# Layernorm gain and shift moved from ScalarE's copies to VectorE, and a fill from ScalarE to GpSimd

## The reference

```python
def _layernorm(x, w, b):
    mu = jnp.mean(x, axis=-1, keepdims=True)
    var = jnp.mean((x - mu) ** 2, axis=-1, keepdims=True)
    return (x - mu) * jax.lax.rsqrt(var + EPS) * w + b
ln1_out = _layernorm(hidden_states, ln1_weight, ln1_bias)
qkv = jnp.einsum('sbh,oh->sbo', ln1_out, qkv_weight)
...
hidden_after_attn = hidden_states + proj_out
ln2_out = _layernorm(hidden_after_attn, ln2_weight, ln2_bias)
x = ln2_out.reshape(-1, H)
logits = jnp.einsum('th,eh->te', x, router_weight)
...
return hidden_after_attn + moe_out
```

## Time and profile before

| | |
|---|---|
| median of 3 runs | 3438.64 us (3434.58 to 3450.35) |
| profiled execution, its own time | 3450.35 us, span 3448.6 |
| mean granted TensorE clock | 0.931 |
| busy over the span | PE 3024.7 us (88%), PEld 1789.5 (52%), DVE 2141.4 (62%), ACT 1497.1 (43%), POOL 1938.9 (56%) |
| last stage | from 3199.2 to the end |

### The profile page before, as it was taken

How to read it: one execution, slowest core, us unless ns; L and a number is a source line. 1 busy time by engine, 2 the same in 40 slices (tenths; PEclk the granted TensorE clock), 3 DMA queues, 4 the chain that set the end, 5 groups by cost and what they waited for, 6 DMA issues and landing times. The chain is left out here.

```text
span 3448.6 us, 62079 instructions
## 1 busy us (share of the span) xinstructions
PE 3024.7 (88%) x19868; PEld 1789.5 (52%) x19868; DVE 2141.4 (62%) x4712; ACT 1497.1 (43%) x2371; POOL 1938.9 (56%) x1254
## 2 busy tenths in 40 slices
PE   4799999999998579985999999999999668886588
PEld 2455555555554567762444444444444347875356
DVE  4577777777775552125676776767765576665563
ACT  2466666666664113324444444444444222211533
POOL 2577787778778220002788888888887222333410
PEclk8899999999998689997999999999999779997789
DMA  6655555555541010000000000000000000000300
GB/s 168 175 195 175 180 188 193 180 176 189 191 171 44 2 49 1 0 34 19 20 19 29 29 19 29 19 29 29 19 29 1 8 1 0 0 0 0 76 1 12
DMA packets 147314, 232.49 MB, mean 67 GB/s; under 512 B 16275, under 2 KB 84955, under 8 KB 147228
## 3 DMA queue, kind: packets, MB, share of 16 engines
q1 hardware_dynamic: 147228, 231.39, 20.9%
HBM read 147.82 MB, written 83.52 MB: 67 GB/s over the span
## 5 line engine op out<-in xcount | busy, mean ns | idle before, releaser
L432 POOL TENSOR_TENSOR sb_a_acc<-sb_a_acc,sb_a_PT 128x1024 f32<-128x1024 f32 x256 | 605.1, 2364 | 34.4 <-ACT sb_a_PT L510 27.0
L593 DVE TENSOR_REDUCE sb_a_mx<-ps_a_A 128x1 f32<-128x512 f32 x768 | 506.5, 686 | 95.7 <-PE ps_a_A L752 90.6
L510 ACT ACTIVATE sb_a_PT<-ps_a_SC 128x1024 f32<-128x1024 f32 (+1 forms) x416 | 425.8, 1023 | 313.3 <-PE ps_a_SC L775 279.9
L1649 POOL TENSOR_TENSOR sb_a_acc<-sb_a_acc,sb_a_PT 128x512 f32<-128x512 f32 (+2 forms) x384 | 487.6, 1270 | 38.7 <-ACT sb_a_PT L1741 12.7
L1741 ACT ACTIVATE sb_a_PT<-ps_a_SC 128x1024 f32<-128x1024 f32 (+2 forms) x256 | 234.3, 916 | 561.5 <-PE ps_a_SC L2012 327.6
L2028 PE MATMUL ps_a_PV<-sb_a_PT,sb_a_XN 128*128 128x512 f32 (+2 forms) x896 | 433.3, 600 | 0.0
L1836 DVE TENSOR_REDUCE sb_a_mx<-ps_a_A 128x1 f32<-128x512 f32 x384 | 256.1, 679 | 266.1 <-PE ps_a_A L1987 265.8
L2012 PE MATMUL ps_a_SC<-sb_a_QX,sb_a_XT 128*128 128x512 f32 (+1 forms) x832 | 397.5, 597 | 0.0
L752 PE MATMUL ps_a_A<-sb_a_KS,sb_a_QS 97*128 97x512 bf16 x768 | 301.1, 393 | 24.2 <-DVE sb_a_QS L585 18.0
L786 PE MATMUL ps_a_PV<-sb_a_PT,sb_a_V 128*32 128x256 f32 (+1 forms) x3328 | 268.2, 394 | 4.2 <-ACT sb_a_PT L510 3.9
L775 PE MATMUL ps_a_SC<-sb_a_QS,sb_a_KS 105*128 105x128 bf16 (+1 forms) x3328 | 258.0, 220 | 13.4 <-DVE sb_a_QS L607 13.4
(11 more groups left out here) (528 smaller groups left out, 5943.0 us busy)
## 6 DMA issues: line engine op xcount, KB each, us to landing
sb_a_C<-in_ctx_dram SPq DMA_DIRECT2D x64, 768.0 KB
a_KD<-sb_a_K SPq DMA_DIRECT2D x192, 256.0 KB
sb_a_KS<-a_KD SPq DMA_DIRECT2D x256, 192.0 KB
a_KD<-sb_a_K SPq DMA_DIRECT2D x192, 144.2 KB, 2.6
sb_a_KS<-a_KD SPq DMA_DIRECT2D x256, 108.2 KB
sb_a_QP<-a_QD SPq DMA_DIRECT2D x6, 384.0 KB, 15.2
sb_a_dn<-n_L_ffn_expert_down_dram SPq DMA_DIRECT2D x1, 2048.0 KB
a_QD<-sb_a_PT SPq DMA_DIRECT2D x3, 512.0 KB, 3.2
```

Of the source, the lines that this page charges most:

```text
L432: pool.tensor_tensor(acc[:, :], first[:, :], PT[slot(a, j)][:, :], ALU.add).then_inc(s["acc"], 1)
L510: act.activation(PT[slot(a, j)][0:n, :], SC[(a + j) % 2][0:n, :], ACT.Exp).then_inc(s["exp"], 1)
L593: v.tensor_reduce(mx[:, p, c:c + 1], A[u % 2][:, :], AXX, ALU.max).then_inc(s["am"], 1)
L1649: pool.tensor_tensor(acc[a][0:m, :], first, PT[u % 4][0:m, HQ * i:HQ * i + HQ], ALU.add).then_inc(s["acc"], 1)
```

## The change

The two norms with gain and shift are now called with them, so that VectorE applies both, over tiles with the token on the partition. There gain and shift run along the row, so the four small tensors become 128 x 128, each row a copy of the vector, and the loads become broadcasts. ScalarE's copies are plain; the second norm's is `norm_scalar` (L237). The zero fill of `vx` moves from ScalarE's start to GpSimd, between the powers of the plain norm and the first one. ScalarE's own wait for `ldw` goes.

```diff
--- before.py
+++ after.py
@@ -2459,7 +2459,7 @@
     KD = KVH * DH
     ctx = ExitStack()
     sb = lambda n, sh, dt=F32: k.sb("a5_" + n, sh, dt, ctx)
-    g1, b1, g2, b2 = (sb(n, [P, 1]) for n in ("g1", "b1", "g2", "b2"))
+    g1, b1, g2, b2 = (sb(n, [P, D]) for n in ("g1", "b1", "g2", "b2"))
     Wqr = sb("Wqr", [P, D])
     Wkvr = sb("Wkvr", [2 * KD, D])
     Wpr = sb("Wpr", [P, D])
@@ -2497,7 +2497,7 @@
         def _(sp):
             sp.dma_start(d["out"].rearrange("b t d -> (b t) d").rearrange("(n p) d -> p n d", p=P), k.x[:, :, :]).then_inc(s["st"], 16)
             for t, n in ((g1, "ln1_weight"), (b1, "ln1_bias"), (g2, "ln2_weight"), (b2, "ln2_bias")):
-                sp.dma_start(t[:, :], d["L1_ffn_" + n].rearrange("(d a) -> d a", a=1)).then_inc(s["ldw"], 16)
+                sp.dma_start(t[:, :], d["L1_ffn_" + n].partition_broadcast(P)).then_inc(s["ldw"], 16)
             sp.dma_start(Wqr[:, :], d["L1_ffn_qkv_weight"][0:P, :]).then_inc(s["ldw"], 16)
             sp.dma_start(Wkvr[:, :], d["L1_ffn_qkv_weight"][P:P + 2 * KD, :]).then_inc(s["ldw"], 16)
             sp.dma_start(Wpr[:, :], d["L1_ffn_proj_weight"]).then_inc(s["ldw"], 16)
@@ -2524,6 +2524,7 @@
                                    fill=MASKED, base=0, pattern=[[-1, B]], channel_multiplier=1).then_inc(s["cm"], 1)
             pool.wait_ge(s["cm"], Q4 + 1)
             norm_pool(k, pool, s["n"])
+            pool.memset(vx[:, :, :, :, :], 0.0).then_inc(s["vz"], 1)
             norm_pool(k, pool, s["n1"])
             pool.wait_ge(s["qc"], NT // 2)
             for g in range(NT):
@@ -2534,9 +2535,6 @@
 
         @block.scalar
         def _(act):
-            act.activation(vx[:, :, :, :, :].rearrange("p n t c d -> p (n t) (c d)"), k.SU[:, :].unsqueeze(1).to_broadcast([P, NT * Q4, P]),
-                           ACT.Copy, scale=0.0).then_inc(s["vz"], 1)
-            act.wait_ge(s["ldw"], 16 * 10)
             act.wait_ge(s["wt"], 1)
             act.activation(WqT[:, :], LG[:, 0:P], ACT.Copy).then_inc(s["wc"], 1)
             act.activation(WpT[:, :], LG[:, P:2 * P], ACT.Copy).then_inc(s["wc"], 1)
@@ -2545,8 +2543,7 @@
             for c in range(NT // 4):
                 act.wait_ge(s["n1"]["turned"], c + 1)
                 act.activation(k.hT[:, :].rearrange("p (t b) -> p b t", b=B)[:, 8 * c:8 * c + 8, :],
-                               banks[c % 2][:, :].rearrange("p (b t) -> p b t", t=T), ACT.Identity, bias=b1[:, :], scale=g1[:, :])\
-                   .then_inc(s["n1"]["copied"], 1)
+                               banks[c % 2][:, :].rearrange("p (b t) -> p b t", t=T), ACT.Copy).then_inc(s["n1"]["copied"], 1)
             for c in range(NT // 4):
                 act.wait_ge(s["q"], 2 * c + 1)
                 act.activation(QT[:, 512 * c:512 * c + 512], SB[c % 2][:, :], ACT.Copy, scale=DH ** -0.5).then_inc(s["qc"], 1)
@@ -2583,10 +2580,7 @@
                 for g in (2 * i + 6, 2 * i + 7):
                     if g < NT:
                         spread(g)
-            for c in range(NT // 4):
-                act.wait_ge(s["n2"]["turned"], c + 1)
-                act.activation(k.hT[:, 512 * c:512 * c + 512], banks[c % 2][:, :], ACT.Identity, bias=b2[:, :], scale=g2[:, :])\
-                   .then_inc(s["n2"]["copied"], 1)
+            norm_scalar(k, act, s["n2"], banks)
             route_scalar(k, act, s, m)
             m.scalar(act, s)
 
@@ -2599,7 +2593,7 @@
             v.wait_ge(s["cm"], Q4 + 1)
             v.tensor_copy(cmb[:, :, :], cmask[0:B, :].unsqueeze(1).to_broadcast([B, H, B])).then_inc(s["cb"], 1)
             v.tensor_copy(rep4[:, :, :], k.ident[0:B, 0:B].unsqueeze(1).to_broadcast([B, Q4, B])).then_inc(s["cb"], 1)
-            norm_vector(k, v, s["n1"], k.hn, Y)
+            norm_vector(k, v, s["n1"], k.hn, Y, g1, b1)
             v.wait_ge(s["wc"], 3)
             v.tensor_copy(WkT[:, :].rearrange("p (k r d) -> p k r d", k=KVH, r=4),
                           WkvT[:, 0:KD].rearrange("p (k d) -> p k d", d=DH).unsqueeze(2).to_broadcast([P, KVH, 4, DH])).then_inc(s["wk"], 1)
@@ -2669,7 +2663,7 @@
             v.wait_ge(s["ldx"], 16 * Q4)
             v.tensor_tensor(k.x[:, :, :], k.x[:, :, :], HP[:, :, :], ALU.add).then_inc(s["xh"], 1)
             v.wait_ge(s["n1"]["turned"], NT // 4)
-            norm_vector(k, v, s["n2"], HP, Y)
+            norm_vector(k, v, s["n2"], HP, Y, g2, b2)
             route_vector(k, v, s, logits, None, m)
             v.wait_ge(s["xh"], 1)
             m.vector(v, s)
```

## The result

| | before | changed |
|---|---|---|
| median | 3438.66 us (3434.58 to 3450.35, 6 runs) | 3459.68 us (3453.13 to 3471.75, 6 runs) |
| ratio | | 1.0057, 95% interval 1.0038 to 1.0078 |
| profiled execution: own time, span | 3450.35, 3448.6 | 3456.78, 3455.0 |
| last stage, first DMA issue to the end | 3199.2 to 3448.6: 249.4 | 3186.2 to 3455.0: 268.8 |

The kernel became slower: its median by 21.0 us, while the ratio of 1.0057 is 19.6 us, with an interval of 13 to 27. The forecast was 3456, in a range of 3446 to 3469. The forecast's chances were counted by a line at 0.5%, and the interval of 0.38% to 0.78% has that line inside. The two spans differ by 6.4 us only, because the profiled execution of before reached the last stage 13.0 us later than that of the changed kernel, in code that the change doesn't touch.

The account below looks back on a forecast made before the run. Bound: a chain through one engine at a time, then TensorE; added microseconds count fully, except in 4.74 us of VectorE idle time. Terms 9.3, 2.9, 3.2, 2.2 sum to +17.6 us; on median 3438.64 that is 3456, range 3446 to 3469.

Parts of the forecast that it names:

- Part 1: Both norms with gain and shift: two added VectorE operations, 4.64 us a call, +9.3 us for two calls.
- Part 2: Tails behind both norms: transposes and copies now wait for the whole shift, +2.9 us second norm, +3.2 first.
- Part 3: Start of last stage: the vx memset on GpSimd blocks VectorE's normalisation, Wpp's copy starts later, +2.2 us.
- Part 4: Last stage's loads: four small loads become 512 bytes a partition, cost 0; up to +1.1 us without the blocking.
- The clock rival: Router behind the second norm: clock does not rise behind the new transposes, +0.9 to +2.1 us, total 3458; chance 0.26.
- TensorE at full clock early: Transposes behind both norms run at full clock, each tail about 1 us less: +15.6 us, 3454; chance 0.09.
- A free memset: Start of last stage: the memset doesn't block VectorE and costs nothing, +15.4 us, 3454; chance 0.10.
- The loads: Last stage's weight loads: wide ones land earlier, idle 4.74 us go; with non-blocking memset +10.7 us, 3449; chance 0.05.

Follow-up runs that it names:

- the fill alone: Kernel before with only the zero fill of vx moved to GpSimd, between the first two powers: 3444.31 us (10 runs), ratio 1.0007.
- the version with warm matmuls on top: Kernel before, expert weights on their own semaphore, 3 and 11 unused matmuls ahead of the first and second norm's transposes: 3437.12 us (11 runs), ratio 0.9985.

## Why the prediction was right, step by step

The forecast was +17.6 us. What its parts 1 to 3 describe are three lengths that hardly depend on the clock; mean of two traces each: Wpp 16.8 to 18.2, norm 1 6.5 to 14.4, norm 2 5.6 to 13.4. Their sum is +17.1 us. Against its terms the traces give +0.1 (part 1), +0.2 (part 2) and -0.8 (part 3), which partly cancel.

- **Part 1, +9.3.** From the normalisation's start to the end of the shift took 3221.43 - 3212.52 = 8.91, less 4.19: 4.72 a call, +9.4. Between L209 and L211 pass 0.11 us, not 0.03.
- **Part 2, +2.9 and +3.2.** Tails behind the shift: 3318.33 to 3322.84 = 4.51 (4.33 said), 3221.43 to 3226.91 = 5.48 (5.5 said). So +3.1 and +3.2. The scattered copy took 1.044 us, said 1.04. The Trainium skill's formula (page "ScalarE: Activation LUTs", section "What ACT_TABLE_LOAD costs") has no term for the output's pattern and would have had 0.61; the contiguous copy, at 0.597, agrees with it. Holding the transposes back with nothing added gave +3.7 and +3.5, with the dearer copies of before.
- **Part 3, +2.2.** The mechanism held, the size was 1.1 to 1.8. The memset took 6.92, not 7.0, and the 16 instructions 10.56, not 11.1. The prediction let all 16 run behind the memset, and said that the end is the same if a tile or two get in first. But the first two, which had started and were blocked, were done 0.15 us behind the memset's end, so only 14 were left: 3.66 us instead of 4.18. Rows 5 name only the longest, 3764 ns; there too two were blocked (3.76 and 3.57 us). The landing in before also varies by 0.5. The later store and reload of hn were covered, as said: attention is 65.8 and 65.7, against 66.0 in the second trace of before.
- **Part 4, 0.** Right within what can be told, about 0.7.
- **The clock rival** came true in part, and dearer than priced. The router was slow in both traces of the changed kernel: 7.0 us at 0.50 throughout, or 0.22 us a matmul, against 5.5 to 6.7 in the prediction, whose rows had only eight matmuls at that clock. That is +2.3 on the means. Projections, attention and experts together give -0.6, in lengths that vary as much from trace to trace. So the last stage is longer by 17.1 + 2.3 - 0.6 = 18.9 us, mean of two traces each. The median's 21.0 and the ratio's 19.6 both lie near that, and the rest is inside the interval. What makes the router slow stays open: it was slow (6.8 in the table, 7.0 to the end of the last matmul) in four of the five traces with gain and shift on VectorE and no warm matmuls, in one of five with the paced transposes of before (the fill alone), and not with the held ones. That it is more often slow in the changed kernel is likely but not shown; neither kind of transposes fixes it.
- **The others.** TensorE at full clock early: seen only when forced, and worth 1.3 us, near the 1 that I gave. A free memset: refuted. The loads: refuted. Wide loads bring no earlier landing that stands out, and with narrow ones the small weights were there after 7.8 us; what landed late were the two expert weights.

The total itself can hardly separate these. It lies nearer to the clock rival's 3458 than to the forecast's 3456, but medians of the same kernel vary by several us, and the 1.1 to 1.8 of the memset were seen in the traces alone. So the terms were right by the traces, and that the total came so near is in part luck.

## What to carry to other kernels

A gain and a shift that ride on a copy are nearly free (0.18 us a copy here, 0.777 against 0.597); on another engine they cost their own time and, if they work on all tiles at once, the overlap of everything behind them as well. An engine that is idle "with 7 us to spare" can still be the wrong place for a fill: ask what it shares with the engine beside it, and which instructions that one runs in those microseconds. Where a wait counts many loads on one semaphore, see which of them the next step needs; here the two big ones weren't needed for another 100 us. The 4.7 us that this gains stand in the stage's lengths; in the total, only the version with warm matmuls on top came out below the kernel before by more than its interval.

## What I had not expected

- The stages ahead of the change varied by 16 us between executions, with the same code: the last stage began at 3183.8 to 3199.6 us over fourteen traces. What causes it is open. In the two traces of before, which differ there by 12.2 us, the stretch from 1128 us to the next stage's first loads (1277.1 against 1270.0) already makes up 7 of it; TensorE's mean granted clock there was 0.76 in the longer and 0.82 in the shorter.
- A memset of 6.92 us blocks two tensor_scalars at once (6.91 and 6.72 us) and a copy (2.42 us), but not a tensor_tensor with both inputs in SBUF (2.29 us, as without it).
- A scattered output (a step of 128 bytes) costs an activation of 128x512 from PSUM 0.45 us, 1.044 against 0.597 us for the plain copy in the same trace.
